# Stage borders of a five-stage network on one core: work moved across them, two stages joined, and the heads' squares on ScalarE

## What is computed

```python
x = x + mamba_and_mlp(conditioned(x))      # in_proj, conv, selective scan, gate, RMS, out_proj; layernorm, MLP 256->1024->256
x = x + experts(pooled(x))                 # softmax pooling, then top 4 of 16 experts, 256->1024->256
# laplace: du = zX*lap_x(x) + zY*lap_y(x) + zR*x*(1-x), and on it differential attention
q, k, v = du @ Wq.T, du @ Wk.T, du @ Wv.T  # 4 heads of 64; each has two softmax maps over 32 features
diff = softmax(q1 k1) - lambda_full * softmax(q2 k2)          # causal; lambda from two exps of dot products
a = diff @ v
a = gamma * a * rsqrt(mean(a*a, over the 64 of a head) + 1e-5) * (1 - LAMBDA_INIT)
x = x + a @ Wo.T
x = x + capacity_moe(subject_linear(x))    # top 1 of 8 experts, 320 slots each, 256->1024->256
```

## Time and profile before

| what | value |
|---|---|
| median of three timed runs | 1443.1 us (1439.0 to 1448.29) |
| profiled execution, its own time | 1443.42 us |
| its span, first to last instruction | 1441.6 us |
| mean granted PE clock | 0.945 |
| busy: PE, PEld | 1320.0 us (92%), 1114.6 us (77%) |
| busy: DVE, ACT, POOL | 921.7 us (64%), 764.4 us (53%), 444.2 us (31%) |
| HBM over the span | 46 GB/s |

### The profile page before, as it was taken

How to read it: one execution, slowest core, us unless ns; L and a number is a source line. 1 busy time by engine, 2 the same in 40 slices (tenths; PEclk the granted TensorE clock), 3 DMA queues, 4 the chain that set the end, 5 groups by cost and what they waited for, 6 DMA issues and landing times. The chain is left out here.

```text
span 1441.6 us, 24764 instructions
## 1 busy us (share of the span) xinstructions
PE 1320.0 (92%) x8550; PEld 1114.6 (77%) x8551; DVE 921.7 (64%) x1715; ACT 764.4 (53%) x1552; POOL 444.2 (31%) x447
## 2 busy tenths in 40 slices
PE   8999699888998789999999999978999898949998
PEld 3465366577894479999999999967788787729997
DVE  5977699846557853354344343366898997445776
ACT  4587867454213156554455555565666675225553
POOL 0000499620000334184035040003322310045885
PEclk9998899989998979999999999989799999979999
DMA  7000000010000023012001000062000000543550
GB/s 248 1 1 8 8 0 2 0 60 1 1 1 1 1 80 154 1 61 113 0 0 58 0 0 0 0 176 69 16 9 8 16 5 10 213 156 119 202 170 18
DMA packets 29293, 71.60 MB, mean 50 GB/s; under 512 B 5539, under 2 KB 14131, under 8 KB 24610
## 3 DMA queue, kind: packets, MB, share of 16 engines
q1 hardware_dynamic: 26914, 64.61, 13.4%
q0 software_dynamic: 2304, 6.03, 1.1%
HBM read 52.51 MB, written 14.19 MB: 46 GB/s over the span
## 5 line engine op out<-in xcount | busy, mean ns | idle before, releaser
L1886 DVE TENSOR_TENSOR ehidl<-hT,ehidh 128x512 fp32r<-128x512 f32 x148 | 132.7, 906 | 140.0 <-ACT ehidh L1869 139.5
L1863 ACT ACTIVATE hT<-ps,eb 128x256 f32<-128x256 f32 x296 | 124.3, 471 | 165.6 <-PE ps L1694 165.6
L2365 PE MATMUL ps<-kp,qz 128*128 128x512 f32 (+3 forms) x384 | 99.8, 390 | 10.3 <-DVE maskb L2447 4.4
L1893 DVE SCALAR_TENSOR_TENSOR X<-ps,wE,X 128x256 f32 x74 | 35.8, 484 | 112.2 <-PE ps L1694 102.7
L2463 DVE TENSOR_REDUCE nmax<-ps 128x1 f32<-128x256 f32 (+7 forms) x128 | 92.0, 753 | 12.1 <-PE ps L2367 10.8
L1869 ACT CAST ehidh<-hT 128x512 fp32r<-128x512 f32 x148 | 91.9, 621 | 4.7
L1694 PE MATMUL ps<-hTh,ew_0h 128*128 x288 | 82.2, 285 | 5.1 <-issue 5.1
L2433 ACT ACTIVATE pr<-ps,nmax 128x256 f32<-128x256 f32 (+7 forms) x86 | 63.5, 741 | 43.2 <-DVE nmax L2463 43.0
L915 POOL TENSOR_TENSOR Gh<-consts,dth 128x1024 fp32r<-128x1024 f32 x16 | 36.1, 2257 | 161.1 <-SPq L771 161.1
L1694 PE MATMUL ps<-hTh,ew_1h 128*128 x304 | 85.6, 282 | 0.0
L1694 PE MATMUL ps<-ew_1h,ehidh 128*128 128x256 f32 x304 | 85.1, 280 | 0.4 <-POOL ew_1l L1806 0.4
(11 more groups left out here) (550 smaller groups left out, 4158.2 us busy)
## 6 DMA issues: line engine op xcount, KB each, us to landing
ew1s<-in_ew_dram SPq DMA_DIRECT2D x8, 1024.0 KB, 4.7
ew2s<-in_ew_dram SPq DMA_DIRECT2D x8, 1024.0 KB, 6.5
fw1s<-in_fw_dram SPq DMA_DIRECT2D x8, 1024.0 KB, 7.2
fw2s<-in_fw_dram SPq DMA_DIRECT2D x8, 1024.0 KB, 9.0
slot_rows<-fill SPq DMA_DIRECT2D x1, 5140.0 KB, 21.3
xr<-slot_rows SPq DMA_DIRECT2D x8, 514.0 KB, 3.9
xT<-in_xT_dram SPq DMA_DIRECT2D x4, 512.0 KB, 7.1
X<-in_x_dram SPq DMA_DIRECT2D x1, 2048.0 KB, 18.2
```

Of the source, the lines that this page charges most:

```text
L1863: nc.scalar.activation(hid[:, f, :], ps[:, f // 2, (f % 2) * JOB:(f % 2 + 1) * JOB], ACT.Gelu, bias=b1[q][:, f:f + 1]).then_inc(k.e_act, 1)
L1886: nc.vector.tensor_tensor(lo[:, f, :], hid[:, f, :], hi[:, f, :], ALU.subtract).then_inc(k.e_lo, 1)
L1893: nc.vector.scalar_tensor_tensor(x, ps[:, DOWN + t, 0:E], wE2[:, bass.ds(e * NT + blk * TILES + t, 1)], x, ALU.mult, ALU.add).then_inc(k.e ...
L2365: nc.tensor.matmul(out[:, at:to], q, k.kp[s % 2][:, f, keys + at:keys + to], start=(part == 0), stop=(part == 1 and to < wide), skip_group ...
```

## The change

1. The first three tiles' turning (AHEAD = 3) moves from outmlp_phase to the end of PE's list in ssd_phase, behind waits for VectorE's and ScalarE's last reads of those PSUM banks. The square of the last tile and the root move the other way: ScalarE does them in outmlp_phase behind its third copy.
2. POOL's two subtractions of 2048 columns become eight of 512.
3. At the end of the projection ScalarE takes the last root, then gelus 0 and 1, then the normalization; the turning and what follows it come one group later (LATE = 4).
4. route_phase and experts_phase become one block, mixture_phase. The route's scratch lies in dead buffers (hT, wop, c2w). What the border had ensured is now waited for: VectorE waits for POOL's low part (r_low) before it writes to hT; PE for r_low, five bias copies before the first job and all eight before each down-projection; ScalarE and VectorE for the first expert's high parts (e_h1) and the table (r_jobs); POOL adds each bias sum behind its copy.
5. Mask, identity and lambda move to laplace_phase, behind the first `low` of VectorE and behind `values(2, 1)` and `low_keys(3, 1)`. POOL places two tiles there instead of three; the third opens its list in attention_phase.
6. The heads' squares leave VectorE. ScalarE makes them, four activations of 64 columns with an accumulator per tile, behind the copies of the first unit of a tile; those of the last two tiles stand in tail_phase, between heads(0) and heads(1). The root of the first 14 tiles is taken at the end of ScalarE's attention, and reciprocal, factor and the first scaling stand on VectorE before the last `collect`.
7. VectorE's two splits of the first capacity expert's weights move behind the border, to the head of capacity_phase.

```diff
 ssd_phase, PE after its last tile; AHEAD = 3, GATED = (0, 1, 2)
+def turn_gated(nc, k, i):
+    for f in range(4):
+        last = nc.tensor.transpose(k.ps[:, GATED[i % 3], f * P:(f + 1) * P], k.yg(i)[:, f, :], k.const("ident"))
+    last.then_inc(k.o_tr, 1)
...
+            pe.wait_ge(k.m_yg, AHEAD)
+            pe.wait_ge(k.m_sz, NT)
+            pe.wait_ge(k.m_xst, NT)
+            pe.wait_ge(k.m_bcu, 2 * NT)
+            for i in range(AHEAD):
+                turn_gated(nc, k, i)
...
             square(NT - 2)
-            square(NT - 1)
-            nc.scalar.activation(k.rms[:, :], ss[:, :], ACT.Sqrt, bias=k.eps[:, 0:1], scale=0.25 / DI)
 outmlp_phase, ScalarE, behind the copy of tile i
+                if i == AHEAD - 1:
+                    nc.scalar.activation(sq[:, :, :], k.yg(NT - 1), ACT.Square,
+                                         accum_out=k.rms[:, NT - 1:NT]).then_inc(k.m_ss, 1)
+                    act.wait_ge(k.m_ss, NT)
+                    nc.scalar.activation(k.rms[:, :], k.rms[:, :], ACT.Sqrt, bias=k.eps[:, 0:1],
+                                         scale=0.25 / DI).then_inc(k.o_sd, 1)
...
             affine(NW - 2)
-            normalize(NW - 1)
+            root(NW - 1)
             for g in range(NW * FB):
+                if g == 2:
+                    normalize(NW - 1)
...
 outmlp_phase, POOL
-                nc.gpsimd.tensor_tensor(parts[1][:, :], whole, parts[0][:, :], ALU.subtract).then_inc(k.p_w, 1)
+                for at in range(0, FB * E, W):
+                    piece = slice(at, at + W)
+                    last = nc.gpsimd.tensor_tensor(parts[1][:, piece], whole[:, piece], parts[0][:, piece], ALU.subtract)
+                last.then_inc(k.p_w, 1)
 mixture_phase (route_phase's lists as route(), in front of those of experts_phase), waits added
+            route()
+            sp.wait_ge(k.r_jobs, 1)
...
+            pool.wait_ge(k.r_jobs, 1)
             rest = later_pairs(pool, "pool")
+            pool.wait_ge(k.e_s1, 1)
             for g in range(NT // 2):
+                pool.wait_ge(k.r_boE, g + 1)
...
+            pe.wait_ge(k.r_low, EB)
+            pe.wait_ge(k.r_boE, 5)
             jobs(pe, "pe", k.pe_rows, k.pe_pairs, job)
...
                 load_next()
+                pe.wait_ge(k.r_boE, NT // 2)
                 pe.wait_ge(k.e_s2, p * 2 + (q + 3))
...
+            act.wait_ge(k.e_h1, 3)
+            act.wait_ge(k.r_jobs, 1)
...
+            dve.wait_ge(k.e_h1, 3)
+            dve.wait_ge(k.r_jobs, 1)
             nc.vector.tensor_tensor(w2[0][1][:, :, :], w2s[0][:, :, :], w2[0][0][:, :, :],
 laplace_phase, POOL
-            for i in range(QZ):
+            for i in range(QZ - 1):
                 place_queries(nc, k, i)
 attention_phase and tail_phase; SQUARED = NT - 2
+def squares(nc, k, act, sq, i):
+    act.wait_ge(k.a_att, i + 1)
+    if i:
+        act.wait_ge(k.a_sq, i)
+    for h in range(HEADS):
+        at = slice(h * 64, (h + 1) * 64)
+        last = nc.scalar.activation(sq[:, at], k.att[:, i, at], ACT.Square, accum_out=k.ms[:, i, h:h + 1])
+    last.then_inc(k.a_sq, 1)
...
                 if n >= 2:
                     turn(n - 2)
+                if n % HEADS == 0 and 2 * HEADS <= n < UNITS:
+                    squares(nc, k, act, sq, n // HEADS - 2)
+            act.wait_ge(k.a_sq, SQUARED)
+            nc.scalar.activation(k.ms[:, 0:SQUARED, :], k.ms[:, 0:SQUARED, :], ACT.Sqrt, bias=k.eps[:, 0:1],
+                                 scale=1.0 / 64).then_inc(k.n_sd, 1)
...
-                dve.wait_ge(k.a_att, i + 1)
-                then(nc.vector.tensor_tensor(sq[:, :], k.att[:, i, :], k.att[:, i, :], ALU.mult))
-                then(nc.vector.tensor_reduce(k.ms[:, i, :], sq[:, :].rearrange("p (h d) -> p h d", h=HEADS), AX.X,
-                                             ALU.add))
...
             collect(NT - 2)
+            head_scales(nc, k, dve, then, 1, slice(0, SQUARED))
+            scale_heads(nc, k, 0)
             collect(NT - 1)
 tail_phase, VectorE (the two splits of its end now open VectorE's list in capacity_phase)
+            scale_heads(nc, k, 1)
             then(nc.vector.memset(base[:, 0, :], 0.0))
...
+            scale_heads(nc, k, 2)
+            head_scales(nc, k, dve, then, 2, slice(SQUARED, NT))
+            scale_heads(nc, k, 3)
```

More of the change, by code:

```diff
@@ L1034, in turn @@
             def turn(i):
-                if i >= 3:
-                    pe.wait_ge(k.o_evac, i - 2)
-                for f in range(4):
-                    last = nc.tensor.transpose(ps[:, TR[i % 3], f * P:(f + 1) * P], k.yg(i)[:, f, :],
-                                               k.const("ident"))
-                last.then_inc(k.o_tr, 1)
+                pe.wait_ge(k.o_evac, i - 2)
+                turn_gated(nc, k, i)
             def project(i):
@@ L1780, in _, with route @@
             pool.sem_inc(k.e_s2, 2)
+            def route():
+                at = slice((NW - 1) * W, N)
+                for j in range(EB):
+                    nc.gpsimd.tensor_copy(k.hTh[:, j, at], k.hT[:, j, at]).then_inc(k.r_hi, 1)
+                for j in range(EB):
+                    pool.wait_ge(k.r_hi, EARLY + j + 1)
+                    nc.gpsimd.tensor_tensor(k.hTl[:, j, at], k.hT[:, j, at], k.hTh[:, j, at], ALU.subtract).then_inc(k.r_low, 1)
+            route()
             def split(s, q, loads):
@@ L2296, with head_scales, scale_heads @@
 UNITS = NT * HEADS
+SQUARED = NT - 2
+def squares(nc, k, act, sq, i):
[6 more added lines that the diff above has]
+    last.then_inc(k.a_sq, 1)
+def head_scales(nc, k, dve, then, roots, tiles):
+    dve.wait_ge(k.n_sd, roots)
+    then(nc.vector.reciprocal(k.ms[:, tiles, :], k.ms[:, tiles, :]))
+    then(nc.vector.tensor_scalar(k.ms[:, tiles, :], k.ms[:, tiles, :], 1.0 - LAMBDA_INIT, None, ALU.mult))
+def scale_heads(nc, k, w):
+    tiles = slice(4 * w, 4 * w + 4)
+    heads = k.att[:, tiles, :].rearrange("p i (h d) -> p (i h) d", h=HEADS)
+    scale = k.ms[:, tiles, :].rearrange("p i h -> p (i h)").unsqueeze(2).to_broadcast([P, 4 * HEADS, 64])
+    nc.vector.tensor_tensor(heads, heads, scale, ALU.mult).then_inc(k.z_sc, 1)
 def attention_phase(nc, k):
@@ L2707, in exponential @@
                 nc.scalar.activation(lg[:, window(w), :], lg[:, window(w), :], ACT.Exp).then_inc(k.z_exp, 1)
-            nc.scalar.activation(k.ms[:, :, :], k.ms[:, :, :], ACT.Sqrt, bias=k.eps[:, 0:1],
+            heads(0)
+            for i in range(SQUARED, NT):
+                squares(nc, k, act, sq, i)
+            act.wait_ge(k.a_sq, NT)
+            nc.scalar.activation(k.ms[:, SQUARED:NT, :], k.ms[:, SQUARED:NT, :], ACT.Sqrt, bias=k.eps[:, 0:1],
                                  scale=1.0 / 64).then_inc(k.n_sd, 1)
-            heads(0)
             heads(1)
```

488 lines of the change are left out of this document (241 added, 247 removed).

## The result

| | median | runs |
|---|---|---|
| kernel before | 1445.69 us | 1439.0 to 1450.33 |
| changed kernel | 1408.84 us | 1406.93 to 1410.49 |

The account below looks back on a forecast made before the run. The prediction took TensorE, busy 92% of the span, as the bound, leaving some 120 us of its idle time. Terms of 4.4 + 3.3 + 2.5 + 3.0 + 0.8 + 4.0 + 2.4 + 2.2 = 22.6 gave 1421 us, range 1411 to 1433.

Parts of the forecast that it names:

- Squares, 4 us: Attention: moving the heads' squares of 14 tiles from VectorE to ScalarE gains 4 us, a third of PE's 12.2 us idle time.
- more from the attention: Rival, attention: PE waits for VectorE in nearly every tile, so 9 us gained instead of 4; total 1414; chance 0.16.
- The price of a block: Attention: one tile's four squares of 64 columns on ScalarE take 1.24 us, 17 us in all, against 63 spare.
- slower: Rival, attention: squares are dear, with two table loads per tile, 14 tiles losing 32 us; total 1457; chance 0.03.
- Ssd to projection, 4.4: Border from ssd to output projection: first projection at 287.9 instead of 292.3, a gain of 4.4 us, bounds 3 and 6.
- POOL's pieces 3.3: Projection: with POOL's subtraction in pieces of 512, VectorE waits 1.1 us at most; 3.3 us gained, bounds 1.5 and 3.7.
- gelus 2.5: End of projection: table load and two gelus ahead of the last normalization remove PE's idle; 2.5 us, bounds 1.5 and 3.
- Fused stage, 3.0: Route and experts in one block: PE's first expert matmul starts earlier, 3.0 us gained, bounds 1.9 and 4.1.
- The rival in which the waits rebuild the border: Route and experts: the fused stage's own waits cost the 3.0 us, total 1424; part of a rival with chance 0.18.
- Laplace to attention, 0.8: Border before the attention: SP's last issues are late next, release at 1008.3 and PE starts then; 0.8 us gained.
- Attention to tail, 2.4: Border before the tail: PE starts 4.0 us earlier, of which 2.4 remain after the tail's first four products; bounds 1.5 and 4.
- Tail to capacity, 2.2: Last border: without VectorE's wide subtracts beside them, POOL's two long scatters take 0.97 us each; 2.2 us gained.

## Why the prediction was wrong

**Squares, 4 us: wrong, 15.2.** This is the step that failed. The text took PE's idle time in the stretch, 189.30 - 177.09 = 12.2, as the upper end of what could be won, and then a third of it, "because PE cannot idle less than nothing in the tiles where it is full". Both halves fail. The upper end was no bound: some 17 us of the stretch ran at half speed, where the same matmuls count as busy for longer, and 7.4 us of busy time went away too. And the third was too little: with VectorE idling for 0.42 us of the 10.90 of the tenth tile, VectorE was the bound of the tile and PE's idle time was made by it. Windows of single tiles would have shown it; the mean over the stretch (PE 177, VectorE 173) hid that the two took turns. PE was full only in the widest tiles, with 0.05 of idle time in the sixth. The theory of "more from the attention" had the mechanism and the place, with 9 us for its size, and got a chance of 0.16. Of the 15.2 us some 11 were waiting and some 4 half clock, by the estimate above, and the half clock was no part of the 4.

**ScalarE's side: right.** The price of a block (1.24 estimated, 1.0 measured) lay in idle time, with no table load; removing it gained nothing. The rival "slower" is refuted by the same run. Doubling it showed how little room was left, against 63 us "to spare" in the prediction.

**Ssd to projection, 4.4: right.** It measured 4.4. The clock's part, which the prediction put at the end of its bounds, is 0.9 in the next stage in one trace.

**POOL's pieces 3.3 and gelus 2.5: right in mechanism, a little small.** They measured 3.5 and 3.2. The stage became 8.9 us shorter against these 5.8; of the rest 0.9 came with the turnings, and 1.3 no run shows alone. What the sum lacked is the clock: two pieces of half speed in that stage before, none after. The prediction priced a clock only at one border.

**Fused stage, 3.0: right in mechanism, its whole worth somewhat smaller.** The two traces give 3.1, and the median of the run with the border back 3.2, which is less than its interval. Over all traces it is 1.8: 3.4 at the start of the loop, within the forecast's bounds, less 1.0 in the loop behind it, which the prediction put at nothing, and 0.6 ahead of VectorE's split, which is scatter as far as the traces show. PE starts 0.48 behind VectorE's split, where the prediction expected 1 to 2. The rival in which the waits rebuild the border is refuted.

**Laplace to attention, 0.8: right that SP was late next,** wrong in the rest. PE starts 0.95 behind SP's end, not 0.3. The two traces give 0.3, and the ten of the changed code together show no gain.

**Attention to tail, 2.4: somewhat small.** PE idles for 1.70 us there, before 6.00 (1217.64 to 1223.64); the tail gave 0.7 back as forecast through its third product (1194.51). 3.6 remain, with 3.4 us at half speed behind the border where there were 10.2.

**Tail to capacity, 2.2: right.** 1.8 in the comparison, 2.0 in the run that undid it. By what the Trainium skill, SBUF — State Buffer, section "Who interferes with whom", marks as inferred, the scatters would not have been held and this term would have been 0. The measurement says otherwise: the scatters of 2.26 and 1.90, twice beside a VectorE subtract with both inputs in SBUF and 0.97 without, were held.

Together, by the two traces: the terms outside the squares were 18.6, and measured 22.1, less 1.0 in stretches that nothing touched; the squares were 4, and measured 15 to 16. Some 2 of the 22.1 are the scatter of single traces, in the fused stage and in Laplace. In 15 to 16 against 4 lies most of the 12 us by which the forecast of 1421 missed 1408.84.

## What to carry to other kernels

When two engines share a stretch and both look nearly full on the mean, cut the stretch into its repeating pieces and ask in each which engine has the least idle time. Here VectorE idled less than PE in six of the 14 tiles (0.42 us against 1.42 in the tenth), though over the whole stretch it idled more (16.6 against 12.2); and 11 of the 14 tiles became shorter by 0.7 us or more when its two small operations went. Idle time of PE is no ceiling for a gain where the granted clock is below 1 in the stretch, because half clock hides in the busy time; add up to half of the busy time in the slow pieces to it. And price a move once more behind itself: 7.5 us less of VectorE's busy time were worth 1 us behind the change, where the 13.1 us less without the squares (172.73 to 159.66) had been worth 15. And before one stretch of two single traces is read as a gain, set it beside the same stretch of every other trace with the same code there: the 3.1 us of the fused stage became 1.8.

## What the runs showed of the hardware

- In the attention the clock fell behind single gaps of PE: before, behind gaps of 1.57, 1.34 and 1.75 us, and in the kernel with the squares on VectorE again behind 1.58, 1.33 and 1.74, at the same places of the stage. Two other gaps of 1.42 and 1.32 had no fall behind them. With two blocks of squares PE idled as much in all, but in gaps of 0.96 at most, and there was no fall. It is no sure rule: without the reciprocals one fall of 3.4 us stands behind gaps of 0.54 and 0.60. What decides was not settled, and the 3.4 us at half speed behind the border of ssd and projection in one of eleven kernels with the same code there, behind a gap of 1.90 that all of them have, belong to the same question.
- The stretch from the route's first matmul to the first expert's took 27.0 to 30.5 us in kernels with the same code there, by the clock and by the arrival of the first weights. ScalarE's first cast of the weights came 22.3 to 25.0 behind the route's first matmul, and the two kernels in which the clock was down for 34 us there took 30.4 and 30.5. A difference of two single traces at this place is uncertain by 3.5 us.
- Beside VectorE subtracts of 2048 columns with both inputs in SBUF, POOL's indirect DMA instructions took 2.26 and 1.90 instead of 0.97, in two kernels; what of their work is held is not shown. And a whole POOL subtract of 2048 columns held a VectorE operation of 4 columns with two SBUF inputs until its end (4.51 and 4.38); beside four pieces of 1.24 that operation took 0.33.
